# One tile in 43 of a graph kernel moves from single-row transfers to GpSimd gathers, and its attention terms into SBUF

## The reference

```python
# attention
xh = (x @ W).reshape(-1, H, C)
alpha = leaky_relu((xh[dst] * a_i).sum(-1) + (xh[src] * a_j).sum(-1), 0.2)
ex = exp(alpha - segment_max(alpha, dst)[dst])
out = segment_sum(xh[src] * (ex / segment_sum(ex, dst)[dst])[..., None], dst)
x = layernorm(x + out)
# three times
hk = relu(concat([h[dst], h[src]], 1) @ linA_w[l].T + linA_b[l])
w = sigmoid(hk @ linB_w[l].T + linB_b[l])
prop = segment_sum(w * h[src], dst)
emb = relu(concat([h, prop], 1) @ lin_w[l].T + lin_b[l])
```

## Time and profile before

| | |
|---|---|
| median of 3 runs | 11323.52 us (11311.4 to 11337.01) |
| the profiled execution, its own time | 11334.84 us |
| its span, first to last instruction | 11333.1 us |
| granted TensorE clock, mean | 0.508 |
| busy: PE / DVE / POOL / ACT | 7017.2 / 4965.6 / 5832.1 / 1564.7 us |
| chain that ended last | SPq 38% (of it L729 30%, L726 5%), issue 32%, unknown queue 13%, DVE 8%, PE 7% |

### The profile page before, as it was taken

The page is one execution under the profiler, slowest core; times in us unless marked ns, Lnnn a source line. Parts: engine busy times, 40 slices in busy tenths (PEclk is TensorE's granted clock), DMA queues, the critical chain, the costliest instruction groups (busy, mean ns, idle before and its releaser), DMA issues.

```text
span 11333.1 us, 183901 instructions
## 1 busy us (share of the span) xinstructions
PE 7017.2 (62%) x33441; PEld 5948.8 (52%) x33442; DVE 4965.6 (44%) x26903; ACT 1564.7 (14%) x6270; POOL 5832.1 (51%) x6174
## 2 busy tenths in 40 slices
PE   4555555555566666666666666666666666666666
PEld 3444444444455555555555555555555555555556
DVE  4555555555554444444443434444444444444444
ACT  2222222222220000000010000000001000000001
POOL 4444444444435555555545555555554555555554
PEclk5555555555555555555555555555555555555555
DMA  4222222222222222222232222222222222222222
GB/s 120 85 84 84 85 84 85 84 85 84 84 81 85 83 82 85 84 85 84 83 90 83 85 84 81 84 85 83 83 83 87 84 82 85 84 83 83 83 82 81
DMA packets 473553, 960.17 MB, mean 85 GB/s; under 512 B 189638, under 2 KB 254454, under 8 KB 472188
## 3 DMA queue, kind: packets, MB, share of 16 engines
q0 software_dynamic: 293376, 801.50, 24.4%
q1 hardware_dynamic: 154172, 136.78, 4.1%
q10 hardware_dynamic: 24932, 12.71, 0.5%
HBM read 919.55 MB, written 30.92 MB: 84 GB/s over the span
## 4 chain that ended last, share of the span: by engine, by line
SPq 38%; issue 32%; another core or an unknown queue 13%; DVE 8%; PE 7%; DVEq 1%; DMA 1%; ACTq 1%; ACT 0%; POOL 0%; POOLq 0%
SPq L729 30%; SPq L726 5%; PE ps L1845 2%; SPq L720 1%; DVE junk L1289 1%; PE ps L1935 1%; PE ps L1834 1%; PE ps L1842 1%; DVEq L1251 0%; DMA acc<-lone_at 0%; PE ps L1945 0%; DVE dg L1332 0%; DVE tt L1414 0%; DVE sel L1259 0%
## 5 line engine op out<-in xcount | busy, mean ns | idle before, releaser
L818 POOL DMA_INDIRECT G<-mp_rows,idx x4116 | 3899.1, 947 | 3392.2 <-ACT idx L916 1769.4
L1935 PE MATMUL ps<-awin,ring 32*128 32x128 f32 x9384 | 2411.9, 434 | 2629.5 <-DVE ring L1611 2188.0
L1935 PEld LDWEIGHTS ps<-awin,ring 32*128 32x128 f32 x9384 | 2083.7, 323 | 2731.8 <-DVE pen L1627 1948.2
L818 POOL DMA_INDIRECT G<-gat_rows,idx x1564 | 1482.7, 948 | 1582.5 <-ACT idx L916 846.1
L1627 DVE TENSOR_TENSOR pen<-ps,G 128x512 f32<-128x512 f32 x1029 | 711.7, 692 | 3406.9 <-remote 2760.5
L1945 PEld LDWEIGHTS ps<-selw,G 128*128 128x128 f32 x8232 | 1834.0, 328 | 393.3 <-issue 393.3
L1945 PE MATMUL ps<-selw,G 128*128 128x32 f32 x8232 | 1972.4, 404 | 0.0
L916 ACT COPY idx<-idx_all 128x4 int32 (+1 forms) x1568 | 300.0, 192 | 6340.0 <-issue 6196.5
L1834 PE MATMUL ps<-sel,ex 128*4 128x32 f32 x3128 | 230.2, 238 | 1430.1 <-DVE tt L1414 1424.8
L1638 DVE SCALAR_TENSOR_TENSOR junk<-pen,ps 128x128 f32<-128x128 f32 x4692 | 1048.3, 270 | 0.1
L1834 PEld LDWEIGHTS ps<-sel,ex 128*4 128x4 f32 x3128 | 161.3, 105 | 1571.2 <-DVE tt L1414 1199.2
(11 more groups left out here) (204 smaller groups left out, 7082.2 us busy)
## 6 DMA issues: line engine op xcount, KB each, us to landing
acc<-mp_rows SPq DMA_DIRECT2D x9216, 1.0 KB
acc<-mp_rows ACTq DMA_DIRECT2D x9216, 1.0 KB
G<-mp_rows,idx POOLq DMA_INDIRECT x4116
ring<-rel_dst SPq DMA_DIRECT2D x98, 512.0 KB
ring<-rel_dst SPq DMA_DIRECT2D x294, 128.0 KB
G<-gat_rows,idx POOLq DMA_INDIRECT x1564
mp_rows<-acc SPq DMA_DIRECT2D x36, 512.0 KB, 3.0
acc<-mp_rows,idx POOLq DMA_INDIRECT x432
```

Of the source, the lines that this page charges most:

```text
L818: pool.indirect_dma_start(out=to[:, t, :], out_offset=None, in_=table, in_offset=bass.IndirectOffsetOnAxis(ap=idx[:, T * u + t:T * u + t + ...
L1935: i = mm(PS[off % 2][:, D * t:D * t + D], selT[0:W, off % 4, P * t:P * t + P], awin[:, off % 4, :], start=True, stop=True)
```

## The change

1. No single rows. `lone`, `LONE_AT` with its DVE operation and its store, `eight_rows`, `fetch_ids` and `slot_and_ids` are gone, on SP and on ACT. POOL gathers all four tiles of every group, so 6256 gathers in place of 6112.
2. SP's loop in a layer holds two offset DMAs per 8 groups and nothing else.
3. The windows of attention terms are no DMAs any more. After the tables are stored, SP reads `gat_si` back once, by 8 DMAs, PE turns the blocks by 8 transposes, and ACT copies them from PSUM into `siw`, a part of `xT`. DVE's `gat_mxs` takes its column there by a register, as a copy into `sm` and an addition: one DVE operation more per group, and no wait for a window.
4. Window bases are rounded down to a multiple of 8, by two small DVE operations at the start.

```diff
-FAR = {19: 0, 21: 2}
-NEAR = {3: 1, 5: 3}
...
+    PH = W // AL
+    NW8 = -(-N // W)
+    BASEMASK = (1 << (N - 1).bit_length()) - AL
...
-    LONE_AT = nc.dram_tensor("lone_at", (NG, P), I32, kind="Internal").ap()
...
+        sirows = selT[:, :, GE // 2:GE].rearrange("p c (b r) -> p c b r", b=2)
+        siw = xT[:, 0:NW8 * W].rearrange("p (a c e) -> p c a e", c=PH, e=AL)[:, :, :, 0]
+        siP = [PS[6 + k][:, 0:2 * NW8].rearrange("p (c a) -> p c a", c=2) for k in range(2)]
...
-        lone = acc[:, 1, 0:LANES * T * TW].rearrange("p (k t c) -> p k t c", k=LANES, t=T)
-        lone_ids = acc[0:1, 1, LANES * T * TW:LANES * (T * TW + P)].bitcast(I32)
...
-        def slot(k0, off):
-
-            return Grows[:, off % U, :, :] if lane(k0, off) is None else lone[:, lane(k0, off), :, :]
...
-            sp.wait_ge(prep, PREP_LONE)
-            sp.dma_start(LONE_AT.rearrange("(q c) p -> q (c p)", c=CQ), lone_at).then_inc(lone_stored, 16)
...
+            for c in range(PH):
+                for b, (lo, hi) in enumerate(((0, P), (P, NW8))):
+                    sp.dma_start(sirows[0:hi - lo, c, b, :],
+                                 SI[AL * H * c + P * lo:AL * H * c + P * hi, :]
+                                 .rearrange("(a r) o -> a (r o)", r=P)).then_inc(si_in, 16)
...
-            def gat_window(k0, off, start):
-                if reached(k0, off, 4):
-                    sp.wait_ge(gat["rhs"], k0 + (off - 3))
-                sp.dma_start(sm[:, off % 4, 0, 0:1], SI[bass.ds(start * H, W * H), :]).then_inc(win_in[off % 4], 16)
-
             def gat_body(k0, stop=U):
-                starts = load_starts(k0)
-                for off in range(stop):
-                    if off % 4 == 0:
-                        gat_offsets(k0, off)
-                    gat_window(k0, off, starts[off])
+                for off in range(0, stop, 4):
+                    gat_offsets(k0, off)
...
-                def eight_rows(n, part):
-
-                    lo = ROWS * part
-                    rows = fresh_registers(sp, ROWS)
-                    sp.load(rows, lone_ids[:, P * n + lo:P * n + lo + ROWS])
-                    for m, reg in enumerate(rows):
-                        at = sp.snap(reg, donate=True, min_val=0, max_val=(N - 1) * TW * 4)
-                        sp.dma_start(lone[lo + m:lo + m + 1, n, T - 1, :].bitcast(U8),
-                                     T1_bytes[:, bass.ds(at, TW * 4)]).then_inc(rows_in[n][l // 2], 16)
-                        sp.free_register(reg)
...
-                def slot_and_ids(k0, off, earlier, ids):
-                    if reached(k0, off, V):
-                        sp.wait_ge(mp["agg"], km + k0 + (earlier + 1))
-                        sp.sem_inc(waited, 1)
-                    sp.wait_ge(sp_ids_in, l * (V * BODIES) + k0 + ids)
-                    sp.sem_inc(waited, 1)
-
-                def lone_rows(k0, off):
-                    if off == 0:
-                        if reached(k0, off, 1):
-                            eight_rows(NEAR[5], 15)
-                        if not (isinstance(k0, int) and k0 == LAST):
-                            fetch_ids(FAR[21], k0, 21)
-                    elif off <= 16:
-                        if off == 1:
-                            slot_and_ids(k0, off, 21 - V, 16)
-                        eight_rows(FAR[21], off - 1)
-                        if off == 16:
-                            fetch_ids(NEAR[5], k0, 5 + V)
-                    else:
-                        if off == 17:
-                            slot_and_ids(k0, off, 5, 32)
-                        eight_rows(NEAR[5], off - 17)
...
+                def body(k0, stop=U):
+                    for off in range(0, stop, 4):
+                        offsets(k0, off)
+
                 body(0)
-                with sp.Fori(1, BODIES) as turn:
-                    body(turn * V)
+                with sp.Fori(1, NG // U - 1) as turn:
+                    body(turn * U)
...
-                    tiles = T if lane(k0, off) is None else T - 1
                     freed = (mp["agg"], km + k0 + (off - U + 1)) if reached(k0, off, U) else None
-                    gather(T1, slot(k0, off), tiles, off, kl + k0 + GR, freed)
+                    gather(T1, Grows[:, off % U, :, :], T, off, kl + k0 + GR, freed)
...
+            act.wait_ge(rel_stored, 32)
+            for k in range(2):
+                act.wait_ge(siw_ps, k + 1)
+                nc.scalar.copy(siw[:, 2 * k:2 * k + 2, :], siP[k]).then_inc(siw_kept, 1)
...
-                def step(k0, off, stop=V, rows=True):
+                def step(k0, off, stop=V):
                     if reached(k0, off, U - LOOKAHEAD):
                         idx_ahead(l + 1, k0, off, stop)
                     if stop == V or off + 1 < stop:
                         keep_window(k0, off + 1)
                     if reached(k0, off, 1) and off - 1 < stop:
                         gate_of(k0, off - 1)
-                    if rows:
-                        lone_rows(k0, off)
...
+            then(v.tensor_single_scalar(baseI[0:QP, :], baseI[0:QP, :], BASEMASK, ALU.bitwise_and))
+            then(v.tensor_copy(baseF[0:QP, :], baseI[0:QP, :]))
...
             def gat_mxs(k0, off, done=gat):
-                m, w = mx[:, off % 4, :], off % 4
-                dve.wait_ge(*done["window"](0, k0, off))
+                m, si = mx[:, off % 4, :], xT[:, bass.ds(base[off], 1)]
                 dve.wait_ge(done["mx"], k0 + (off + 1))
-                v.tensor_tensor(m[:, 1:2], m[:, 0:1], sm[:, w, 0, 0:1], ALU.add).then_inc(done["mxs"], 1)
+                v.tensor_copy(sm[:, off % 4, 0, 0:1], si).then_inc(done["mxs"], 1)
+                v.tensor_tensor(m[:, 1:2], m[:, 0:1], si, ALU.add).then_inc(done["mxs"], 1)
...
+            pe.wait_ge(si_in, 16 * 2 * PH)
+            for c in range(PH):
+                for b, (lo, hi) in enumerate(((0, P), (P, NW8))):
+                    i = tr(siP[c // 2][:, c % 2, lo:hi], sirows[0:hi - lo, c, b, :], ident[0:hi - lo, 0:hi - lo])
+                if c % 2:
+                    i.then_inc(siw_ps, 1)
...
-                for landed in done["rows"](0, k0, off):
-                    pe.wait_ge(*landed)
...
-                        i = mm(PS[2 + off % 2][:, 0:W], slot(k0, off)[:, t, 0:D], selw[:, off % 4, W * t:W * t + W],
+                        i = mm(PS[2 + off % 2][:, 0:W], Grows[:, off % U, t, 0:D], selw[:, off % 4, W * t:W * t + W],
```

More of the change, by code:

```diff
@@ L8 @@
 from contextlib import ExitStack, contextmanager
-from itertools import count
 import numpy as np
@@ L28 @@
 H = 4
+AL = 8
 U = 8
 V = 4 * U
-ROWS = 8
-FAR = {19: 0, 21: 2}
-NEAR = {3: 1, 5: 3}
 NB = 128
@@ L359, in rows_landed @@
             return gathered[off % U], 8 * k0 + (stage * whole + 64 * (off // U + 1))
-        def window_landed(stage, k0, off):
-            whole = 16 * (NG // 4 - (off % 4 == 3))
-            return win_in[off % 4], 4 * k0 + (stage * whole + 16 * (off // 4 + 1))
         def offsets_landed(stage, k0, off):
             return offs_in[off // 4 % 2], 2 * k0 + (stage * 2 * NG + 16 * (off // U + 1))
[L370 to L374, removed]
-        def slot(k0, off):
-            return Grows[:, off % U, :, :] if lane(k0, off) is None else lone[:, lane(k0, off), :, :]
[L380 to L404, removed]
-        gat = dict(ahead=True, rows=all_landed, window=window_landed, offsets=offsets_landed, **gat_sems)
-        mp = dict(ahead=True, rows=all_landed, window=window_landed, offsets=offsets_landed, **mp_sems)
+        gat = dict(ahead=True, rows=rows_landed, offsets=offsets_landed, **gat_sems)
+        mp = dict(ahead=True, rows=rows_landed, offsets=offsets_landed, **mp_sems)
         x_total = sem("x_total")
@@ L419, in one_by_one @@
         def one_by_one(sems, w):
-            return dict(ahead=False, rows=lambda stage, k0, off: [(x_rows, w * 64 + 64)],
+            return dict(ahead=False, rows=lambda stage, k0, off: (x_rows, w * 64 + 64),
                                    window=lambda stage, k0, off: (x_win, w * 32 + 32),
@@ L686, in _ @@
                 sp.sem_inc(waited, 1)
-                sp.dma_start(relbc, REL[bass.ds(at.g, 1), :].rearrange("o e -> (o e)")
-                             .partition_broadcast(P)).then_inc(x_win, 16)
-                sp.dma_start(sm[:, 0, 0, 0:1], SI[bass.ds(at.node * H, W * H), :]).then_inc(x_win, 16)
+                for half in range(2):
+                    sp.dma_start(relbc[half * (P // 2):(half + 1) * (P // 2), :],
+                                 REL[bass.ds(at.g, 1), :].rearrange("o e -> (o e)")
+                                 .partition_broadcast(P // 2)).then_inc(x_win, 16)
             def load_x(turn, off):
@@ L760, in body @@
-                def body(k0, stop=V):
-                    for off in range(stop):
-                        if off % 4 == 0:
-                            offsets(k0, off)
-                        if stop == V or off == 0:
-                            lone_rows(k0, off)
```

(13 more changed lines are left out.)

78 lines of the change are left out of this document (12 added, 66 removed).

## The result

| | before | after |
|---|---|---|
| median | 11326.56 us (4 runs) | **10703.46 us** (10659.56 to 10735.81, 4 runs) |
| the profiled execution | 11334.84 us | 10735.81 us |

The ratio is 0.9448, 95% interval 0.941 to 0.9487: 5.5% faster, where slower had been forecast at 11,810 us. The time lies just inside the lower edge of the range (10,650 to 12,250), near the 10,700 of the relief rival.

A forecast was written before the change was run, and what follows sets the result against it. Waits set the pace: POOL gathers in bursts, with a restart and a standstill. Layers +455 (middle of +250 and +660), windows +30 and prologue +3 made +488, forecast 11,810 us against the median; 8-in-10 range 10,650 to 12,250.

The forecast's parts named there:

- relief rival: SP's and ACT's queues set the pace; removing them outweighs 144 gathers: 10,700 to 11,130 us, value 10,930, chance 0.28.
- The restart of 3.22 us through ACT's gate and copy: Layers: from consumers' first signal, through L1627, dot products, gate and copy, to POOL's next gather, 3.22 us.
- ACT without rows: Layers: ACT waits before its gate during the standstill; two-group cycles take 14.57 us, +660 us including the additional gathers.
- the freeze: While POOL bursts, DVE gets no word of PE's product until after the last gather; 2760.5 us before L1627.
- The sign set for the forecast: Layers: POOL's gap before a burst grows from 2.9-3.6 to about 4.5-5.8 us, still released by ACT's copy.
- gain end: Layers: if cycles with three groups come, 19.57 us each, 6.52 a group, -240 us.
- SP without rows: Layers: offsets come early, up to 406.5 us of DVE's wait goes; none of it counted in the forecast.
- the cover of "remote": DVE, released earlier from offsets, would stand longer before L1627, whose 2760.5 us of "remote" hides that gain.
- 144 gathers: POOL in the layers: 180 us of pure issue, or +250 us at 1.734 us each.
- Windows and prologue: One more DVE operation per group, taken as +30 us; start-up DMAs and transposes, taken as +3 us.
- The freeze going: Rival: the standstill ends with SP's and ACT's DMAs, POOL runs without pause: 8,220 us, partly up to 10,600; chance 0.13.

The follow-up runs named there:

- e1: Kernel before with no single rows, POOL gathering all tiles, attention windows still DMAs: 10500.21 us, ratio 0.9388 to before (11177.88 us) on that chip.
- f1: The changed kernel again, on another chip where the kernel before takes 11184.72 us: 10498.52 us, ratio 0.9400.
- f3: Changed kernel with ACT's copy of node numbers 6 groups ahead in place of 4: 10429.53 us, ratio 0.9328 to before (11184.72 us).
- e3: Kernel before with ACT's single rows only; SP issues offsets alone, POOL gathers 72 tiles more: 10803.03 us, ratio 0.9671 to before.
- e2: Kernel before with SP's single rows only; ACT issues none, POOL gathers 72 tiles more: 10770.04 us, ratio 0.9640 to before.
- e4: Kernel before with single rows still issued but read by nobody, POOL gathering all tiles: 11320.22 us, ratio 1.0123 to before (11177.88 us).
- f4: Kernel before with single rows issued but not read, POOL gathering everything, on another chip: 11313.28 us, ratio 1.0125 to before (11184.72 us).
- f2: Kernel before with no single rows, windows still DMAs, on another chip: 10505.18 us, ratio 0.9390 to before (11184.72 us).
- e5: The changed kernel itself, on a chip where the kernel before takes 7989.26 us: 8167.19 us, ratio 1.0221.
- e6: Kernel before with no single rows, windows still DMAs, where before takes 7989.26 us: 8171.68 us, ratio 1.0225.

## Why the prediction was wrong

**The restart of 3.22 us through ACT's gate and copy was the step that failed.** It stood under "ACT without rows", made every cycle of two groups 14.57 us and with it the +660. Measured in layer 1 of after (medians), a cycle of two groups takes 12.33 us: 8.75 of burst, 2.85 from the last issue to DVE's first addition, 0.73 from there to POOL's next gather. None of these cycles ends on ACT's copy: 44 of them and more end on PE's `agg`, which frees a slot, the rest on "remote". The numbers lay ready, since ACT had copied them for a third group inside the burst. I had assumed that ACT always stands in front of the gate that the freeze holds, with no numbers ready for POOL. Where the copy does end the wait, after 59 of the 82 bursts of 12, the restart is 3.47 us: the chain was sized about right, but it stands behind three groups and not behind two. The sign set for the forecast, gaps of 4.5 to 5.8 us ended by ACT's copy, did not come either: in the waits of the result's chip shown above those gaps average 4.2 us (259.2 / 62) and the ones ended by a slot 2.1 (152.3 / 73). I had also read the attention stage as the model of a layer without rows. It was not: it kept its 3047 us and its cycles of eight gathers, while the layers changed theirs.

**Cycles of three groups were the gain end, and are the rule.** I had put 19.57 us on them; they take 18.47 (17.94 on the other standstill chips, e1, f1 to f3), since DVE goes on 1.25 us after the last issue (median) where I had 2.60. I had said that the third copy comes at 8.8 us, behind the start of the freeze. In the rows above the three copies come at 4508.98, 4511.29 and 4514.89, so the third comes 5.9 us after the first, just before DVE's wait begins at 4515.13. DVE's first signal had come at 4504.39, before the last gather of that burst (4505.19), so "it comes only after the last gather" was too strict a reading of the earlier trace rows. Both kinds of cycle take 6.2 us a group, where the forecast had 7.29 and its gain end 6.52.

**SP without rows was counted at nothing, under the cover of "remote".** The cover was no cover: "remote" did not take up what the offsets gave back, it fell by 361 us itself. I had read its 2760.5 us from one of two groups of rows. e3 against before takes SP's rows away and gains 375 us although 72 gathers are added; e2 gains 408 by ACT's. The relief rival had both of its pieces right in kind: offsets late by 406.5 us, copies late behind ACT's rows. It priced the offsets and left the copies to a cycle of three groups; the two reliefs overlap, 408 + 375 = 783 us alone against 678 together. That its 10,700 lies beside the measured 10,703 is in part luck: it added 406 us for offsets on top of a cycle of 19.57 us that in fact takes 18.47, and did not say how much of the one is in the other.

**144 gathers.** The term was 1.734 us each, +250. Measured in the old regime it is 142 and 129 us (e4, f4), below 1.25 each; that part of the issue falls into POOL's idle time is my reading of it. On unbroken chips it is 178 us, the pure issue term. There the forecast's sign is right, and there POOL's issue time is the bound. The rule of the Trainium skill, "DMA: Bandwidth & Descriptors", section "Issuing engines are not separate DMA queues", would have given about 0; the runs give 129 to 178 us, so the measurements decide against it here.

**Windows and prologue.** +30 and +3 were taken. The attention stage moved by -2 us, f1 and f2 differ by 7 us with intervals that overlap, and e5 and e6 by 4. No cost and no gain above these few us; that the added copy would stop POOL's gathers did not show.

**The freeze going** had 0.13 and did not come from the change: 3027.9 us of "remote" remain without a single row. That rival's POOL-bound time of 8220 us is nearly the 8167 us of an unbroken chip, by another cause than the one it named.

**What to have done.** The trace of before held the sign: SP never waits, ACT's copy is 8 us late. I let a model of the cycle with three assumed parts outweigh these two rows. The model had no check of its own, since in no row was ACT free of DMAs while PE had the layers' work.

## What to carry to other kernels

An engine's queue that never waits may be the bound even if its issues are short: price what stands behind them (offsets, index copies) before the work they save. In this kernel, moving work from the gather engine to other queues paid where that engine's issue was the bound, and cost where waits were: the same 18,432 single rows are worth 2.2% on one chip and cost 5.5 to 6.1% on another. If two chips give different traces, look at which wait ends last on each before tuning for one.

## What the hardware showed that I had not expected

The chips of these jobs fall into two kinds for this program: before takes 11,327 us in the result and 11,178 and 11,185 on two further chips, and 7979 to 8000 us on three, all at a granted clock of 0.51. In the changed kernel single instructions last the same on both (a gather 945 ns, the addition 692 and 691 ns), and so does PE's work in a layer (1718 and 1738 us). The difference is all waiting: "remote" before DVE's addition, 3027.9 us on one kind and none on the other. In the rows shown it begins inside a row of gathers and DVE's waits last 7.40 and 7.05 us.

ACT's copy of PE's `win` shows best what is late, since it waits for PE alone; first after, then e5:

```profile
L938 ACT COPY awin<-ps 32x128 f32<-32x128 f32 x1173 | 298.0, 254 | 5108.9 <-remote 3396.7
L938 ACT COPY awin<-ps 32x128 f32<-32x128 f32 x1173 | 297.9, 254 | 1997.5 <-PE ps L1786 1997.5
```

In 276 of 1173 steps of after such a wait for "remote" ends more than 3 us after PE's `win` has ended, in e5 in none. So it is the signal of a finished product that comes late on the one kind of chip. Why it does was not shown.

On a standstill chip some DMA issues of ACT beside gathers are slow as well, 7.62 us for eight rows in this row of e3, against 2.70 in the step before it; SP's 11 rows from 5008.00 on took 9.02 us in before. On the other kind of chip no trace has such rows, so how long they take there is not known. The two steps of e3:

```profile
4004.90 2.70 ACTq L1060 DMA_DIRECT2D acc<-mp_rows  x8
...
4008.68 7.62 ACTq L1060 DMA_DIRECT2D acc<-mp_rows  x8
```
